# A graph network's last stage: one row tile in eight, not one in four, scaled on GpSimd

## What is computed

```python
edge_index = jnp.stack([src, dst])
x = _layernorm(x + _L0_gnn_ref(x, L0_gnn_W, L0_gnn_b, edge_index), axis=-1)
x = _layernorm(x + _L1_gnn_ref(x, edge_attr_512, src, dst, ...), axis=-1)
```

```python
out = node_feat + out                      # out: summed messages @ Wo.T + bo
mean = out.mean(axis=0)
var = jnp.mean(jnp.square(out - mean), axis=0)
out = (out - mean) * jax.lax.rsqrt(var + EPS) * gamma + beta
```

## Time and profile before

| What | us |
|---|---|
| Median of three runs | 1349.71 |
| The profiled execution's own time | 1352.15 |
| Its span, first to last instruction | 1350.1 |
| First product of the last stage's loop on VectorE | at 1218.36 |
| Its last row statistics | at 1343.92 |

### The profile page before, as it was taken

One profiled execution on the slowest core, in us unless ns is written; L12 is line 12 of the kernel. 1 busy time (PEld: TensorE's weight loads), 2 busy tenths in 40 slices (PEclk: granted clock), 3 DMA queues, 4 the chain that ended last, 5 costly groups with the idle time before them and its releaser, 6 DMA issues. The chain is left out here.

```text
span 1350.1 us, 21775 instructions
## 1 busy us (share of the span) xinstructions
PE 1279.4 (95%) x6374; PEld 1029.7 (76%) x6374; DVE 1078.2 (80%) x2035; ACT 637.4 (47%) x1243; POOL 814.1 (60%) x752
## 2 busy tenths in 40 slices
PE   7889889999999699999999999999999999879997
PEld 5767778888888588888888888888888888754333
DVE  7576648999999325788988888888888888887887
ACT  3565647888888312323332332223223333257886
POOL 3666336676766533566656666666655555668885
PEclk9999999999999799999999999999999999978999
DMA  8888867788886523434444444444444443659986
GB/s 289 286 270 259 259 228 253 257 260 273 256 264 204 179 63 101 129 112 125 126 128 129 127 138 140 133 133 140 140 140 140 140 135 98 217 177 382 295 295 224
DMA packets 128300, 257.95 MB, mean 191 GB/s; under 512 B 21459, under 2 KB 21907, under 8 KB 128114
## 3 DMA queue, kind: packets, MB, share of 16 engines
q1 hardware_dynamic: 97490, 175.31, 39.4%
q0 software_dynamic: 29920, 80.38, 20.6%
q10 hardware_dynamic: 832, 1.57, 0.3%
HBM read 197.18 MB, written 73.60 MB: 201 GB/s over the span
## 5 line engine op out<-in xcount | busy, mean ns | idle before, releaser
L208 PE MATMUL ps<-w_lo,w_hi 128*128 128x512 f32 (+2 forms) x1140 | 415.9, 365 | 4.0 <-DVE w_lo L1430 1.4
L209 PE MATMUL ps<-w_hi,w_lo 128*128 128x512 f32 (+2 forms) x1140 | 410.2, 360 | 0.0
L210 PE MATMUL ps<-w_hi 128*128 128x512 f32 (+2 forms) x1140 | 410.1, 360 | 0.0
L208 PEld LDWEIGHTS ps<-w_lo,w_hi 128*128 128x128 f32 x1140 | 217.1, 190 | 36.2 <-DVE w_lo L1484 2.4
L210 PEld LDWEIGHTS ps<-w_hi 128*128 128x128 f32 x1140 | 216.9, 190 | 32.4
L209 PEld LDWEIGHTS ps<-w_hi,w_lo 128*128 128x128 f32 x1140 | 217.2, 191 | 29.7
L1268 POOL TENSOR_TENSOR acc_x<-acc_x,node_rows 128x512 f32<-128x512 f32 x72 | 114.5, 1590 | 84.5 <-DMA node_rows<-x_table 80.3
L923 POOL TENSOR_TENSOR node_y<-node_z,node_x 128x512 f32<-128x512 f32 x79 | 102.6, 1298 | 72.1 <-DVE node_agg L1021 36.9
L208 PE MATMUL ps<-w_lo,agg_hi 128*128 128x512 f32 x316 | 131.5, 416 | 1.5 <-DVE agg_lo L992 1.5
L209 PE MATMUL ps<-w_hi,agg_lo 128*128 128x512 f32 x316 | 124.8, 395 | 0.0
L210 PE MATMUL ps<-w_hi,agg_hi 128*128 128x512 f32 x316 | 124.7, 395 | 0.0
(11 more groups left out here) (278 smaller groups left out, 2875.1 us busy)
## 6 DMA issues: line engine op xcount, KB each, us to landing
node_x<-in_x SPq DMA_DIRECT2D x79, 256.0 KB, 4.1
x_table<-node_x SPq DMA_DIRECT2D x79, 256.0 KB, 2.2
node_rows<-x_table SPq DMA_DIRECT2D x79, 256.0 KB, 8.4
coef_all<-coef_table SPq DMA_DIRECT2D x38, 512.0 KB, 7.1
edge_part<-part SPq DMA_DIRECT2D x40, 256.0 KB, 4.0
out_dram<-rows_over_w_lo SPq DMA_DIRECT2D x40, 256.0 KB, 6.4
node_x<-in_ea SPq DMA_DIRECT2D x38, 256.0 KB, 4.1
msg_table<-dst_rows_and_msg SPq DMA_DIRECT2D x38, 256.0 KB, 5.0
```

Source lines behind the costliest of these rows:

```text
L208: pe.matmul(to, left[0], right[1], start=first, stop=False, skip_group_check=onto)
L209: pe.matmul(to, left[1], right[0], start=False, stop=False, skip_group_check=onto)
L210: return pe.matmul(to, left[0], right[0], start=False, stop=last, skip_group_check=onto)
```

## The change

`by_pool(j)` is true for tiles 2, 10, 18, ..., 74 instead of 2, 6, 10, ..., 78: 10 tiles instead of 20. The other ten (6, 14, ..., 78) are multiplied by VectorE.

```diff
         def by_pool(j):
-            return j % 4 == 2
+            return j % 8 == 2
```

## The result

The changed kernel takes 1354.38 us (median of 20 runs, 1349.24 to 1364.72), the kernel before 1349.72 beside it (20 runs, 1343.71 to 1356.23): a ratio of 1.0044 [1.0031, 1.0058]. It is **slower**, by 4.7 us, where 3.3 us less was forecast, and it lies outside the range given. The profiled execution took 1364.72 us and is the slowest of the twenty, so its loop shows the loss at its largest.

A forecast was written before the change was run, and what follows sets the result against it. GpSimd's unbroken stream was taken as the bound. Moved products +3.15, pace and holds of before -6.6, holds left +0.1 gave -3.3 us: 1349.71 to 1346.4 us, range 1343.4 to 1352.6.

The forecast's parts named there:

- the bias, 0.14 long, is just ahead of the product and not held: From tile 42 on: VectorE's bias at 1.28 us, GpSimd's product 1.33 to 1.47 after slot 13's kind of product begins.
- the 0.1 us that the sum took for holds: Loop, nine remaining GpSimd products: only tile 10's catches a bias, 0.4 us long, costing 0.1 us in all.
- the prediction's outer bound: Loop, tiles 10 to 74: all nine GpSimd products hold a bias whole, 9 us lost.
- The price of a hold: VectorE's bias held by a GpSimd product: at most a whole product, 1.28 us, about 1.0 lost.
- length less 0.31: Rule for VectorE's loop: a held bias costs its length less 0.31 us, read from two cycles.
- the holds come back: Rival, late loop: last five products hold biases, 1351.4 us; all nine, 1355.3 us; chance 14%.
- When GpSimd's lead is used up: Loop: GpSimd gains 0.6 us per eight tiles, then follows ScalarE's copies from tile 42 on.
- +0.35 us for a product moved: VectorE's loop: each moved product lengthens its slot from 1.19 to 1.54 us; nine slots, +3.15 us.
- The tail: Tile 78, after the loop: its moved product fills a 0.62 us wait for TensorE, costing zero; uncovered, 0.6 us.
- The waits for gathers: VectorE's loop: three products waiting for gathers, 2.9 us in all, would go.
- the transfers are the pace: Rival, gathers: issued earlier they land no earlier, the 2.9 us of waits stay, 1349.3 us; chance 13%.
- -6.6 us "to GpSimd's pace": VectorE's loop: 6.6 us lost to GpSimd, about 2.9 at transfers and 3.7 at held biases, would be regained.

The follow-up runs named there:

- the gate: Changed kernel with a tiny GpSimd memset, which the product waits for, between the gather and the product: 1347.18 us, 0.9978 of the kernel before.
- the execution with six: The changed kernel measured again, unedited, with a second profile: 1356.65 us, 1.0062 of the kernel before; its profiled execution took 1356.55 us.
- the run with the scalar bias: Changed kernel with the bias L2094 as one tensor_scalar per tile, rstd read as a scalar operand: 1345.47 us, 0.9968 of the kernel before.

## Why the prediction failed, point by point

**The step that failed is "the bias, 0.14 long, is just ahead of the product and not held".** The order was right: the bias does come ahead of the recorded product, by 0.57 to 0.61 us even, more than the 0.05 to 0.19 worked out. The conclusion was wrong, since a part of the product has begun by then, 0.34 us after the start of the gather ahead of it. The runs with the gate and with 32 partitions, in which the bias comes at the same place and passes, show that it is this early part that holds it. The trace before did not contradict the step, and it could not support it either. One bias of before began in the gather ahead of a product, 0.32 us into it, and was not held (GpSimd, then VectorE):

```profile
1230.37 1.00 POOL L1943 DMA_INDIRECT rows_over_w_lo<-msg_table,last_edge  x1 [0.30 <-issue]
1231.39 1.28 POOL L1950 TENSOR_TENSOR fin_u_more<-fin_u_more,fin_scale_row 128x512 f32<-128x512 f32 x1
```

```profile
1230.69 0.14 DVE L2094 SCALAR_TENSOR_TENSOR fin_bias<-fin_mv,fin_rstd 128x2 f32<-128x2 f32 x1
```

Another began 0.13 ahead of such a gather, and the rest that came near began after the product's start. No bias of before lay between 0.32 and 1.02 us, the place to which the step's own sum led. So the 0.1 us that the sum took for holds had no row under it; nine holds, the prediction's outer bound, are what the first profiled execution shows.

The Trainium skill has the parts of this ("Perfetto Trace Analysis", section "GPSIMD Engine Instruction" and section "DMA Instruction — SWDGE (GPSIMD)"): GpSimd is eight cores of 16 partitions each, every one with a queue of its own; a start is reported when the first reads; and the first two write a gather's descriptors. Six cores would then be free for a product while two still work on the gather. The run with 32 partitions agrees as far as it goes: with the product on partitions 0 to 31 alone, which those two would do, no bias was held. No run shows the cores themselves. The Trainium skill adds there that the separate queues usually don't matter in practice; if they are the cause, they cost 1.56 us a time here.

**The price of a hold** was the second error. The prediction held the longest possible one to be a whole product, 1.28 us, 1.0 lost. With the early start it spans 1.9 us, and 1.56 are lost; the rule "length less 0.31" itself stood.

**The rival "the holds come back" is what happened**, with its place right (slots 8m + 5, once GpSimd follows the copies), its reason wrong (no order was turned round) and its price too low: five at 1.0 gave 1351.4 us; six at 1.56 in place of five would have given 1346.4 + 9.4 = 1355.8, and the execution with six took 1356.55. The sign that the prediction named for its failure, biases of 0.8 us or more in those slots late in the loop, appeared. The prediction had given this rival 14%.

**When GpSimd's lead is used up.** "From tile 42 on" was close where the loop ran undisturbed: in the second profile the holds begin with tile 34. (The lead also grows more slowly than worked out: by the prediction's rows gathers follow each other by (1256.05 - 1252.09) / 3 = 1.32 us, not 1.30, so it is 0.5 us per eight tiles, not 0.6.) It was far off in the first: there a bias 0.72 us into the gather (1228.62 - 1227.90) was caught in slot 5, and from the gather of tile 16 on GpSimd waited for copies. A hold delays VectorE, the banks and with them the copies (the copy of tile k waits until PE has used tile k - 12, not k - 11: there are 12 buffers), so it spends the lead itself, and then the phase is fixed: product to product 1256.50 - 1242.74 = 13.76 us on GpSimd, 13.75 on VectorE. I treated the holds as single accidents; in both profiled executions they are a state in which the two streams stay.

**+0.35 us for a product moved** was right: 0.36 by the run without any GpSimd product. The tail was right, too: from slot 77's bias to the last row statistics it is 1356.09 - 1353.27 = 2.82 us, and 1343.92 - 1341.05 = 2.87 before. TensorE wasn't waited for in the loop.

**The waits for gathers** went, as predicted, and not only because holds gave the gathers time: the run with the scalar bias has none either. The rival "the transfers are the pace" is out.

**-6.6 us "to GpSimd's pace"** was right in size (with the bias that isn't held the change reaches 110.30 where 109.8 was predicted) and half wrong in its cause. 3.0 of it was holds, which need no lighter GpSimd: with another form of the bias, the kernel before gets them back by itself, while its GpSimd keeps its cycle of 6.42 us. So what the change alone could bring was the 3.4 to 3.6 us of waiting for gathers, and its products cost 3.15. Even without holds the forecast gain of 3.3 was not the change's.

## What to carry to other kernels

When an instruction is moved against another that it can block, look for the phase in which the two will settle, not for the mean; when one stream follows the other, a bad phase can repeat to the end of the loop, as it did here. In this kernel a GpSimd product issued right behind a gather, with its own rows already landed, is to be taken as begun in part about 0.7 us before its recorded start. Where a VectorE instruction of 0.14 us is exposed to that, change its operands or make the product wait for it: each of the two took this kernel below both versions (0.9968 and 0.9974 of the time before), and the first did nearly as much, 0.9975, without the change.

## What was not expected of the hardware

- A GpSimd product behind a gather begins in part 0.7 us before the start that the trace gives it, by the release of a bias 0.40 us before that start. With the product on partitions 0 to 31 alone no bias was held; that the early part is the one on the other partitions is inferred from this.
- The hold isn't for the whole instruction. A bias slips in between the early part and the rest: 0.20 us with 32 columns, 0.40 with 128, but 1.61 with 384 and 1.9 with 512. The Trainium skill ("SBUF — State Buffer", section "Who interferes with whom") words it as a lock for the whole instruction; the long products agree, the short ones don't.
- While the holds repeat in the changed kernel, the gather ahead of the colliding product starts late, with 0.47 to 0.52 us of idle time instead of 0.30, and 0.06 to 0.09 us behind the end of VectorE's reciprocal (1241.64 to 1241.70 above). It keeps the bias, which follows the reciprocal, at 0.42 to 0.45 us into the gather, and may be what holds the phase so firmly. That the reciprocal causes it is not shown: no run took it away, and in the kernel before three gathers start while one runs (one at 1239.25, in the reciprocal of 1239.13 to 1239.29).
